# GpSimd's wait for the preceding unit's landing moved from a unit's second row gather to its third

## What is computed

```
xpad = jnp.pad(x, ((0, 0), (PAD, PAD), (PAD, PAD), (0, 0)))
...
def g(yy, xx):
    valid = (yy >= 0) & (yy < Hin) & (xx >= 0) & (xx < Win)
    v = img[jnp.clip(yy, 0, Hin - 1), jnp.clip(xx, 0, Win - 1)]
    return v * valid[..., None]
...
samp = (v00 * (1 - wx) + v01 * wx) * (1 - wy) + (v10 * (1 - wx) + v11 * wx) * wy
return jnp.einsum('hwpc,hwp->hwc', samp, m)
```

## Time and profile before

| | us |
|---|---|
| median of 3 runs (14348.79 to 14365.49) | 14355.92 |
| the profiled execution, its own time | 14375.56 |
| its span | 14373.9 |
| GpSimd busy, of the span | 9445.4 (66%), 9221 instructions |
| VectorE busy, of the span | 9751.2 (68%) |
| TensorE matmuls busy | 8550.2 (59%) |
| ScalarE busy | 4857.6 (34%) |
| DMA queue of the row gathers | 604.57 MB, 14.9% of 16 engines |

### The profile page before, as it was taken

The page is one execution under the profiler, slowest core; times in us unless marked ns, Lnnn a source line. Parts: engine busy times, 40 slices in busy tenths (PEclk is TensorE's granted clock), DMA queues, the critical chain, the costliest instruction groups (busy, mean ns, idle before and its releaser), DMA issues. The chain is left out here.

```text
span 14373.9 us, 109977 instructions
## 1 busy us (share of the span) xinstructions
PE 8550.2 (59%) x32544; PEld 4159.5 (29%) x32544; DVE 9751.2 (68%) x9864; ACT 4857.6 (34%) x13537; POOL 9445.4 (66%) x9221
## 2 busy tenths in 40 slices
PE   6773657356664558446664558446664558555667
PEld 3241324122332324222332224222332324222223
DVE  6755976569764886569765886569765986544443
ACT  3232533145321543145321543145322543122221
POOL 0005777777777777777777777777777777777771
PEclk7886778667887679767887679767887679777778
DMA  1011111321133111421133111421133112432221
GB/s 69 9 31 58 52 58 56 102 78 52 58 84 105 52 50 58 110 79 52 58 83 104 52 56 52 113 76 52 58 83 105 52 59 60 106 111 94 72 78 48
DMA packets 905628, 1001.99 MB, mean 70 GB/s; under 512 B 697681, under 2 KB 707921, under 8 KB 893074
## 3 DMA queue, kind: packets, MB, share of 16 engines
q0 software_dynamic: 294912, 604.57, 14.9%
q1 hardware_dynamic: 610066, 389.88, 8.8%
HBM read 814.38 MB, written 179.39 MB: 69 GB/s over the span
## 5 line engine op out<-in xcount | busy, mean ns | idle before, releaser
L133 POOL DMA_INDIRECT gat<-corner_tables,idx x9216 | 9445.0, 1025 | 4626.3 <-issue 2484.6
L170 DVE TENSOR_REDUCE dcn<-gat 128x32 f32<-128x1152 f32 x1024 | 2161.7, 2111 | 320.0 <-ACT gat L150 287.2
L150 ACT ACTIVATE gat<-gat,wts 128x32 f32<-128x32 f32 x8752 | 1906.9, 306 | 962.1 <-DMA gat<-corner_tables,idx 961.2
L164 DVE TENSOR_TENSOR gat<-gat,wts 128x1152 f32<-128x1152 f32 (+3 forms) x1024 | 1094.5, 1069 | 1672.9 <-DMA gat<-corner_tables,idx 1559.7
L797 PE MATMUL PS<-hc,ident 128*128 128x512 f32 (+2 forms) x4096 | 1963.9, 639 | 233.9 <-DVE hc L841 192.6
L864 DVE TENSOR_TENSOR_SCAN hs<-dA,PS 128x1024 f32<-128x1024 f32 x672 | 1531.9, 2280 | 45.5 <-ACT dA L814 18.1
L797 PEld LDWEIGHTS PS<-hc,ident 128*128 128x128 f32 x4096 | 1018.4, 281 | 858.7 <-issue 477.5
L1152 ACT ACTIVATE E<-PS,nmax 128x1024 f32<-128x1024 f32 x512 | 570.5, 1114 | 945.2 <-DVE nmax L1209 774.0
L1073 PE MATMUL PS<-ident,E 128*128 128x128 f32 x4096 | 600.9, 294 | 427.7 <-ACT ET L1142 226.9
L841 DVE TENSOR_TENSOR hc<-hs,PS 128x1024 f32<-128x1024 f32 x672 | 802.0, 1193 | 0.8 <-issue 0.8
L1742 PE MATMUL PS<-late_M,wp 128*32 128x512 f32 x4480 | 632.3, 715 | 267.0 <-DVE wp L1783 184.6
(11 more groups left out here) (251 smaller groups left out, 11481.2 us busy)
## 6 DMA issues: line engine op xcount, KB each, us to landing
gat<-corner_tables,idx POOLq DMA_INDIRECT x9216
corner_tables<-xp SPq DMA_DIRECT2D x1024, 64.0 KB, 2.2
D<-in_dist_dram SPq DMA_DIRECT2D x8, 4096.0 KB, 13.8
keep_scratch<-X SPq DMA_DIRECT2D x15, 2048.0 KB, 11.3
weighted<-M SPq DMA_DIRECT2D x56, 512.0 KB, 2.8
late_M<-weighted SPq DMA_DIRECT2D x7, 4096.0 KB
wqkv<-in_qkv_w_dram SPq DMA_DIRECT2D x8, 3072.0 KB, 11.5
X<-keep_scratch SPq DMA_DIRECT2D x12, 2048.0 KB, 15.9
```

What stands on the lines that cost most here:

```text
L133: nc.gpsimd.indirect_dma_start(bd.gat[n % self.NG][:, k * 4 * CG:(k + 1) * 4 * CG], None, bd.rows, bass.IndirectOffsetOnAxis(ap=bd.idx[:, ...
L150: ins = nc.scalar.activation(block, block, ACT.Copy, scale=weights[:, i:i + 1])
L164: nc.vector.tensor_tensor(v, v, wv, ALU.mult).then_inc(self.prod, 1)
L170: nc.vector.tensor_reduce(bd.dcn[m % 2][:, g * CG:(g + 1) * CG], gat[:].rearrange("p (k c) -> p c k", c=CG), AX.X, ALU.add).then_inc(self. ...
```

## The change

The condition under which GpSimd waits for the unit before is k == 2 in place of k == 1:

```diff
@@ -123,7 +123,7 @@
         for i, (n, k) in enumerate(rows):
             m, g = n // G, n % G
-            if k == 1 and n:
+            if k == 2 and n:
                 pool.wait_ge(self.gathered[(n - 1) % self.NG], 16 * KP * ((n - 1) // self.NG + 1))
             if k == 0 and n >= self.NG:
                 pool.wait_ge(self.summed, n - self.NG + 1)
```

## The result

| | before | after |
|---|---|---|
| median of 4 runs, us | 14352.35 | 13920.53 |
| lowest to highest | 14342.80 to 14365.49 | 13913.76 to 13926.31 |
| profiled execution, own time | 14375.56 | 13926.31 |

The change makes the kernel 3.0% faster: the ratio is 0.9702, with a 95% interval of 0.969 to 0.9714. A later repeat gave 0.9703. The forecast was 13,830 us and lay 90 us too low; the range of 13,750 to 14,080 held the time. Between the two profiled executions the gain is 449.2 us, where the sum said 530.

The account below looks back on a forecast made before the run. GpSimd's stream of gather rows was taken to set the pace for 12.9 of 14.4 ms. Of 620 us saved there, 89 + 342 + 99 = 530 us pass on: 14,356 - 530, about 13,830 us, range 13,750 to 14,080.

Parts of the forecast that it names:

- The wait itself: GpSimd's landing wait, one row later, would mostly be met already: 400 us off GpSimd's stream, late landings staying.
- The held row: GpSimd's waiting second row, lengthened by VectorE's multiply, would become plain, with 0.04 us left on the next: 220 us.
- E + 1.62: E is the end of a unit's ninth row; landing known and VectorE's multiply started 1.62 us later.
- Rival A: The multiply waits for the row it starts in, so the held row only moves on: 14,046 us, chance 0.13.
- Where the next wait comes: Next late: VectorE in the scan, with a wait for the sum holding GpSimd, and GpSimd's 1.25 us a row elsewhere.
- First round: 1160 to 2758 us: of 92 us gained on GpSimd, 3 go to the scan and 89 pass on.
- last round: 12415 to 14079 us: of 112 us gained on GpSimd, 99 pass on.
- six loop rounds: In each, GpSimd gains 72 us, of which 57 pass on: 342 us for six.
- the 13 us: Part of the last round's 112 us gain, counted as lost ahead of the power stages.
- this unit: One more unit of GpSimd lead from the scan, removing 11.6 us of VectorE's wait behind it; net loss 7 us.
- Rival B: VectorE's stages set the pace sooner, in attention and preparation, so only 270 us pass on: 14,086 us, chance 0.08.
- Rivals C and D: C: landing tied to the issue behind it, no change, 14,356, chance 0.05; D: younger rows delay landing, 14,556, 0.04.

Follow-up runs that it names:

- ring of six: The changed kernel with six buffers for units in place of five (NG = 6): 13861.50 us, ratio 0.9673 to the kernel before.
- combined kernel: The changed kernel with the landing wait at a unit's last row and six buffers together: 13744.54 us, ratio 0.9574 to the kernel before.

## Why the prediction was right in the main and 81 us off

**The wait itself: right.** 400 us were forecast, 585 - 186.5 = 399 came: 321 of it in waits of under 2.5 us, for landings that had been just too late.

**The held row: right in kind, 220 forecast, 173 came.** The rows' busy time fell by 200.7 us. But the median row also reads 0.944 us in place of 0.947, and 9216 x 0.003 = 28 us of the fall are that. It isn't the change's doing: in the repeat of the changed kernel the median row reads 0.947 again, and the rows are 187.2 us shorter. Counted one by one, the rows that start inside a gather multiply are 467.1 us longer than plain ones before, 294.0 after: 173 less. The second rows alone gave 245 of it, as forecast (269 to 24). But third rows took back 32, and the others together 40: 792 of the 1024 multiplies now start inside a row, 511 did before, and the row behind pays for it.

I took 0.04 us as what stays on the next row. A unit of the change, at the place of the earlier trace rows, shows more. The multiply starts at 5830.58:

```profile
5830.42 0.94 POOL L133 DMA_INDIRECT gat<-corner_tables,idx  x1 [0.30 <-issue]
5831.67 1.09 POOL L133 DMA_INDIRECT gat<-corner_tables,idx  x1 [0.30 <-issue]
```

The ninth row of the unit had ended at 5828.87, so the multiply comes at E + 1.71, not 1.62. That is 0.16 us inside the second row, not 0.06, and 0.15 stays on the third. The prediction had taken E + 1.62 from single units; over all units that VectorE waited for, the median is E + 1.66 before and E + 1.69 after. Over all full-size multiplies, those that start within the first 0.1 us of a row leave 0.01 to 0.08 on the next, those at 0.5 us some 0.46, and those at 0.9 some 0.88. Rival A, in which the multiply would wait for the row that it starts in, falls: here the multiply starts and the row goes on beside it. The Trainium skill (SBUF — State Buffer, "Who interferes with whom") has the shared ports locked for a whole instruction. A row behind a multiply agrees; a multiply that starts 0.16 us inside a row, takes its plain 1.36 us and leaves that row at 0.94, does not.

**Where the next wait comes: right in kind, not priced.** The sum's wait was named as the next one; it took 140 us of GpSimd's time (174.5 - 106 x 0.30 = 142.7, less 18.0 - 50 x 0.30 = 3), where the sum had only a net loss of 7 in each loop round. And it wasn't all harmless: the ring of six took 61 us of it away and was 43 us faster. By the signs that the prediction named: landing waits 204.2 us in 59 waits (about 200 in some 60 forecast), rows 200.7 us shorter (220), VectorE's gather waits down by 598.9 us (500), the scan 536.2 us (537). In all, GpSimd's last gather starts 449.7 us earlier (13628.67 against 14078.37), and the program ends 449.2 us earlier.

**What passes on, by rounds.** First round 87.9 us (89 forecast), last round 105.9 us (99), and each of the six loop rounds 42.8 (57). So the whole miss is in the loop rounds, 6 x 14.2 = 85 us. In one of these GpSimd and VectorE wait after as follows (5811.2 to 7377.9 us, beside the earlier trace rows):

```profile
DVE gat L164 <- DMA gat<-corner_tables,idx: 75.2, 13, 11.5
...
POOL gat L133 <- DVE dcn L170: 29.4, 16, 10.5
...
POOL gat L133 <- DMA gat<-corner_tables,idx: 23.3, 8, 6.1
```

GpSimd's landing waits fell as forecast, 70 to 21. VectorE's gather waits fell by 66.8 us, and the round by only 45.6 (1612.3 to 1566.7). The time of rows held by gather multiplies fell by 17, not 23.

That the last round came near is in part luck. GpSimd gained 104 us there (42 of landing waits, 57 of held rows, some 6 of grants), not 112, but the 13 us set aside as lost ahead of the power stages were not lost.

**The step that failed**, with 11.6 of the 14.2 us by which a loop round missed, is "this unit removes 11.6 of the 12.0 us that VectorE waits between 6914 and 7064 us". The wait did go:

```profile
DVE gat L164 <- DMA gat<-corner_tables,idx: 0.4, 1, 0.4
```

That is the same stretch after, 6714 to 6864 us. But the stretch is 150.2 us long before and 150.0 after. Its last part, a group norm and the start of attention, ends with a wait for TensorE's projections. The first operation of attention, in the kernel before and in the change:

```profile
7064.30 0.69 DVE L1201 TENSOR_TENSOR kk<-PS,cols 128x512 f32<-128x512 f32 x1 [17.67 <-PE PS L1047]
```

```profile
6864.22 0.69 DVE L1201 TENSOR_TENSOR kk<-PS,cols 128x512 f32<-128x512 f32 x1 [29.47 <-PE PS L1047]
```

The idle time did not go away, it changed its name: 17.67 + 11.6 = 29.3 us. That part takes 52.6 us before, 52.7 in the change and 52.6 to 52.7 in the ring of six, with the wait at the last row and in the combined kernel. The prediction took a gather wait of VectorE as time on the path, without asking what ends last behind it. The other 2.6 us of a loop round aren't traced to one step.

**Rival B** had a share of truth. Attention fell from 319.7 to 309.4 us and stayed at 309.4 with the ring of six and in the combined kernel, so that is its own pace (VectorE has no gather wait left in it); I had put it at 304 for 26 units. The other parts of the round that became shorter are the steps (122.0 to 110.4), the preparation (205.7 to 195.4), and "gram" (104.1 to 99.0). The preparation still lost to a full ring: in it GpSimd stands 10.5 us for a sum, and VectorE waits 8.8 us for gathers. With a sixth buffer these gather waits are gone, and the stage is at 186.6. **Rivals C and D** fall: all 1024 second rows start after the plain 0.30 us, and with a row issued behind it a landing is known at E + 1.69 in the median, not E + 2.87.

## What to carry to other kernels

Where one event releases two engines that can hold each other up, the wait costs more than its own length: move it by a step, and look in the timeline at what starts beside what. Where a wait only guards against too much in flight, put it as late as that guard allows; here the wait at the last row of a unit gives 0.9642 where the third gives 0.9703, and with one buffer more the ratio is 0.9574. And before a removed wait is counted as gain, read the next operation of the waiting engine: if it waits for a third engine in the same stretch, the time only changes its name.

## What was not expected of the hardware

- A row gather that starts while VectorE's multiply of two SBUF tiles runs is held (1.94, 1.51 us in place of 0.94): in the change, 352 rows of over 1.2 us started inside a gather multiply, and they ended 0.82 us behind that multiply's end (0.81 to 0.82 from the 5th to the 95th percentile). The row inside which the multiply starts is not held, and the multiply keeps its 1.35 us. The row behind is longer by the multiply's offset into the row less 0.02 us, to within 0.02, for offsets from 0.15 us on. A reduction beside a row does nothing: 1189 rows that started inside a unit's sum lasted 0.944 us in the median, 0.947 at the 95th percentile. So 292 us of added work made a kernel 230 us faster.
- Gathers that land during a large fetch on SP's queue are late by up to 9 us, with the mean rate at 345 GB/s, and younger rows in flight don't make it worse: with the wait at the last row VectorE's longest gather wait is 12.3 us, with it at the third 12.4. That the large fetch is the cause is read from the two standing side by side in time; no run moved the fetch, so this stays open.
- The median row takes 0.944 us in some executions and 0.947 in others of the same kernel (the change and its repeat). Summed over 9216 rows that is 28 us, and it belongs to no edit. Why is open.
